# Re-ordering a hand-written five-engine schedule: loads, rotations and the last output unit of a fused attention and expert kernel

## The reference

```
h = layernorm(x)
q, k = rope(bf16(h @ Wq.T)), rope(bf16(h @ Wk.T))         # one head, width 128
o = sum over keys <= query of exp(q . k / sqrt(128))      # one number a row
a = relu(o @ fc1_w.T + fc1_b) @ fc2_w.T + fc2_b           # 1 -> 16 -> 128
x = x + layernorm(a)
h = layernorm(x)
y = relu(h @ W1[1] + b1[1]) @ W2[1] + b2[1]               # 128 -> 256 -> 128
x = x + layernorm(y)
```

## Time and profile before

| | us |
|---|---|
| median of 3 runs | 92.8 |
| lowest, highest | 92.72, 94.83 |
| the profiled execution | 92.89 |
| its span in the trace | 91.1 |

### The profile page before, as it was taken

How to read it: one execution, slowest core, us unless ns; L and a number is a source line. 1 busy time by engine, 2 the same in 40 slices (tenths; PEclk the granted TensorE clock), 3 DMA queues, 4 the chain that set the end, 5 groups by cost and what they waited for, 6 DMA issues and landing times.

```text
span 91.1 us, 1515 instructions
## 1 busy us (share of the span) xinstructions
PE 82.2 (90%) x439; PEld 49.2 (54%) x443; DVE 78.9 (87%) x210; ACT 67.7 (74%) x190; POOL 56.8 (62%) x79
## 2 busy tenths in 40 slices
...
GB/s 42 289 256 272 270 179 161 207 146 67 164 11 85 122 23 0 102 17 0 0 0 0 0 0 7 0 0 0 0 7 7 115 0 0 0 0 89 286 262 169
DMA packets 11852, 7.64 MB, mean 84 GB/s; under 512 B 819, under 2 KB 10948, under 8 KB 11844
## 3 DMA queue, kind: packets, MB, share of 16 engines
...
## 4 chain that ended last, share of the span: by engine, by line
PE 54%; ACT 23%; SPq 9%; DMA 5%; issue 2%; DVE 1%; POOL 1%; POOLq 1%; DVEq 0%
ACT psum L549 18%; PE psum L719 17%; PE psum L791 15%; PE psum L745 10%; DMA x_s<-x 5%; PE psum L711 5%; SPq L324 4%; PE psum L770 3%; SPq L304 2%; ACT fc L562 1%; PE psum L764 1%; ACT qk L501 1%; ACT h1T L518 1%; PE psum L749 1%; PE psum L781 1%
## 5 line engine op out<-in xcount | busy, mean ns | idle before, releaser
L485 POOL TENSOR_TENSOR rstd<-ve,half_neg 128x4 f32<-128x4 f32 (+1 forms) x36 | 35.7, 997 | 27.9 <-DVE ve L350 17.7
L549 ACT ACTIVATE psum<-psum 128x1024 f32<-128x1024 f32 (+7 forms) x48 | 36.5, 761 | 0.6 <-PE psum L749 0.2
L745 PE MATMUL psum<-qk_r 128*128 128x512 bf16 (+3 forms) x76 | 19.7, 346 | 1.8 <-ACT psum L549 1.3
L719 PE MATMUL psum<-cols_n,wqk 128*128 128x512 f32 (+1 forms) x36 | 16.9, 561 | 0.0
L719 PE MATMUL psum<-cols_n,w_c 128*128 128x512 f32 (+1 forms) x36 | 15.9, 551 | 0.0
L791 PE MATMUL psum<-w_c,hid 128*128 128x128 f32 x128 | 15.8, 276 | 0.0
L791 PEld LDWEIGHTS psum<-w_c,hid 128*128 128x128 f32 x128 | 15.3, 192 | 0.7 <-issue 0.3
L745 PEld LDWEIGHTS psum<-qk_r 128*128 128x128 bf16 x80 | 6.6, 97 | 12.9 <-ACT psum L549 6.3
L501 ACT ACTIVATE cols_n<-psum 128x512 f32<-128x512 f32 (+1 forms) x12 | 6.3, 528 | 8.2 <-PE psum L711 8.2
L711 PE MATMUL psum<-ident,rows_n 128*128 128x128 f32 x64 | 10.1, 276 | 0.9 <-DVE rows_n L344 0.9
L711 PEld LDWEIGHTS psum<-ident,rows_n 128*128 128x128 f32 x64 | 7.4, 141 | 5.9 <-issue 3.3
...
## 6 DMA issues: line engine op xcount, KB each, us to landing
x_s<-x SPq DMA_DIRECT2D x7, 256.0 KB, 4.3
qk_swap<-qk SPq DMA_DIRECT2D x14, 128.0 KB, 2.3
out<-x_s SPq DMA_DIRECT2D x7, 256.0 KB, 2.4
table<-tables SPq DMA_DIRECT2D x3, 256.0 KB, 3.8
x_s<-x SPq DMA_DIRECT2D x2, 128.0 KB, 3.2
w_f<-w SPq DMA_DIRECT2D x2, 128.0 KB, 3.7
table<-tables SPq DMA_DIRECT2D x2, 128.0 KB, 4.4
out<-x_s SPq DMA_DIRECT2D x2, 128.0 KB, 2.0
```

Source lines behind the costliest of these rows:

```text
L485: ready[k].done(eng.tensor_tensor(rstd[:, g, STAT_SLOT[k], t], ve[:, g, STAT_SLOT[k], t], half_neg[:, 0:tiles], ALU.pow), n)
L549: exps.done(eng.activation(area, area, ACT.Exp, scale=scale_qk, accum_out=sums[:, g, s, j:j + 1]), n, j, s)
L719: made[name].done(eng.matmul(bank_of(name, n)[:, 0:tiles * P], weight, cols_n[:, g, c], start=True, stop=True), n)
L745: mm = eng.matmul(psum[:, own[0] + i, 0:width], query, qk_r[:, g0 + c, 1, 0:width], start=True, stop=c < gb)
```

## The change

- Front unit 1 (second half of group 0) is no longer swapped by PE (`rot.1`) but by two transfers (`swap.1`). `rot.0` stays.
- A new list `OUTS` gives the units of the last stage (`y`, `bias`, `stat5`, `eps5`, `rstd5`, `ys`, `out`, `store`). It is BACKS, with unit 8 (two tiles) cut into units 8 and 9 of one tile. A `y` unit waits for the copies of the BACKS unit that holds its tile.
- `load_fc`, until now two issues on ACT's queue, goes to SP's queue, and the small loads take other places in it.
- STEPS is a new order for all engines, with other banks, and with some shared steps on other engines. `rot` apart, all arithmetic is the same.
- Branches for one tile to a bank are added to `net_pair`, `xs`/`ys` and `fc2`; no unit of the new STEPS gives a bank to one tile of several, so none of them runs.

```diff
+OUTS = [(0, 0, 4), (1, 0, 4), (4, 0, 4), (5, 0, 4), (2, 0, 4), (6, 0, 4), (3, 0, 4), (7, 0, 2), (7, 2, 1), (7, 3, 1)]
...
-load_x.0 blank.9#7 blank.1.128#7 load_x.3 repeat.0 load_x.4 mask.0 load_fc.0.A load_b1.0 load_wqk.0 stat1.0 load_x.1
-eps1.0.A rstd1.0 load_x.8 stat1.3 load_w2.0 norm1.0.D eps1.3.D load_x.6 stat1.4 tr1.0#0 rstd1.3 load_x.5 wqk.0#1
-eps1.4.D +tr1.0.A stat1.1 load_table.0 fc.0#2 rstd1.4 +wqk.0.A norm1.3.D load_b2.0 blank.1.128#7 q.0#1 eps1.1.D
-load_table.1 rstd1.1 tr1.3#0 norm1.4.D load_table.2 k.0#3 +tr1.3.A stat1.8 tr1.4#4 load_x.7 w2mean.0 stat1.6 q.3#0
-load_x.2 eps1.8.P +q.0.A stat1.5 +k.0.A eps1.6.P k.3#5 +tr1.4.A rstd1.6 cos.0.D w2.0 norm1.1.D rot.0#4 q.4#3 +k.3.D
-fcmean.0 norm1.6.P +q.3.A sin.0.D b2mean.0 tr1.1#1 swap.3 k.4#5 eps1.5.A rstd1.8 rope.0.D +q.4.A cos.3.D +tr1.1.A
-tr1.6#4 +k.4.A stat1.2 scores.0.1.0#1 norm1.8.P k.1#3 +tr1.6.A swap.4 scores.0.0.0#5 stat1.7 q.1#0 eps1.2.A +k.1.A
-q.6#4 rstd1.2 +fc.0 cos.4.D load_table.3 sin.3.D tr1.8#3 load_table.4 exp.0.1.0 k.6#6 rstd1.5 load_w1.0 rope.3.D
...
-stat5.1.D store.0 store.5 h1.7#2 store.3 eps5.1.D stat5.6.D rstd5.1 h0.7#3 store.4 +h1.7.D y.8#0 eps5.6.A +h0.7.D
-rstd5.6 out.1 y.7#3 stat5.8.A out.6 eps5.8.P store.1 stat5.7.A rstd5.8 eps5.7.D out.8 store.6 rstd5.7 store.8 out.7
-store.7
+load_x.0 blank.10#7 blank.1.384#7 load_x.3 repeat.0 load_x.6 mask.0 load_w2.0 load_wqk.0 stat1.0 load_x.4 eps1.0.A
+rstd1.0 stat1.3 load_x.8 load_x.5 eps1.3.D stat1.6 rstd1.3 load_fc.0 w2mean.0 norm1.0.D eps1.6.A wqk.0#0 norm1.3.D
+load_x.1 tr1.0#1 +wqk.0.A load_table.0 stat1.4 rstd1.6 blank.1.256#7 +tr1.0.A tr1.3#2 load_x.2 q.0#1 eps1.4.D stat1.8
++tr1.3.A rstd1.4 load_x.7 k.0#0 +q.0.A norm1.6.D blank.1.128#7 load_table.1 k.3#2 eps1.8.A w2.0 norm1.4.D load_b1.0
+q.3#1 load_table.4 +k.3.A rstd1.8 stat1.1 load_w1.0 stat1.5 eps1.1.A tr1.4#3 +q.3.A tr1.6#2 norm1.8.D +tr1.4.A swap.3
+fc.0#4 stat1.2 eps1.5.P +tr1.6.A rstd1.5 q.4#3 fcmean.0 load_b2.0 eps1.2.A cos.3.D +k.0.A tr1.8#2 load_table.2 cos.0.D
+k.4#0 +tr1.8.A stat1.7 norm1.5.P k.6#1 +q.4.D +k.4.A rstd1.1 sin.3.D +fc.0 swap.4 k.8#2 rstd1.2 rope.3.D rot.0#0
+b2mean.0 tr1.5#3 load_table.3 cos.4.D eps1.7.A b2.0 scores.2.3.0#4 +k.6.D norm1.2.P +tr1.5.A q.6#5 +k.8.A sin.0.D
+scores.2.0.0#1 norm1.1.P exp.2.3.0 scores.2.1.0#3 +q.6.D q.8#6 rstd1.7 exp.2.0.0 sin.4.D exp.2.1.0 swap.6 tr1.1#5
...
+eps3.0.D +trz.2.D rstd3.0 w1.0#1 cos.7.D exp.1.2.0 scores.5.2.0#67 +w1.0.D sin.7.P scores.4.3.1#2 x1.0 exp.5.2.0
...
+scores.4.2.1#2 eps3.7.D +trz.0.D scores.4.0.1#3 h0.3#4 rstd3.7 +hT.1 rope.7.P x1.7 scores.4.1.0#67 exp.4.0.1 exp.4.2.1
++h0.3.D fc2.1#15 exp.4.1.0 scores.5.0.0#23 stat3.1.D scores.5.1.1#4 h1.3#0 exp.5.1.1 eps3.1.D stat4.7 exp.5.0.0
+rstd3.1 sum.4.D scores.6.3.1#67 +h1.3.D h1.0#4 b2split.0 exp.6.3.1 x1.1 hT.4#0 scores.6.3.0#23 +hT.4 +h1.0.D
...
++h1.5.A eps5.3.P out.1 out.4.P trz.8#1 h0.6#3 +trz.8.A +h1.7.D +h0.7.D rstd5.3 y.5#1 store.4 +h0.6.A store.0 +h1.6.A
+out.2.P out.3 y.6#4 stat5.5.A store.2 store.3 store.1 eps5.5.A rstd5.5 h1.8#6 stat5.6.D h0.8#3 +h1.8.A out.5 y.7#2
+eps5.6.P +h0.8.A rstd5.6 y.8#3 store.5 stat5.7.D y.9#1 out.6 eps5.7.P stat5.8.A rstd5.7 stat5.9.A eps5.8.A eps5.9.A
+store.6 out.7 rstd5.8 rstd5.9 store.7 out.8 store.8 out.9 store.9
...
+OUT_STEPS = {"y", "bias", "stat5", "eps5", "rstd5", "ys", "out", "store"}
...
+        back_of = {(g, j): n for n, (g, j0, tiles) in enumerate(BACKS) for j in range(j0, j0 + tiles)}
...
-            g, j0, tiles = (FRONTS if name in FRONT_STEPS else BACKS)[n]
+            g, j0, tiles = (FRONTS if name in FRONT_STEPS else OUTS if name in OUT_STEPS else BACKS)[n]
...
-                    taken["h0"].wait(eng, n)
-                    taken["h1"].wait(eng, n)
+                    taken["h0"].wait(eng, back_of[g, j0])
+                    taken["h1"].wait(eng, back_of[g, j0])
```

More of the change, by code:

```diff
@@ L16 @@
 BLOCK = 32
-PAIR = 2 * BLOCK
 HIDDEN = 256
@@ L38 @@
 STEPS = """
[L39 to L73, removed]
@@ L74 @@
-+trz.8.A +h0.6.A rstd5.3 ys.4 h1.8#2 +h1.6.A h0.8#7 trz.7#0 out.0.P out.3 +h0.8.A y.6#6 +trz.7.A +h1.8.A out.4.P
-stat5.1.D store.0 store.5 h1.7#2 store.3 eps5.1.D stat5.6.D rstd5.1 h0.7#3 store.4 +h1.7.D y.8#0 eps5.6.A +h0.7.D
-rstd5.6 out.1 y.7#3 stat5.8.A out.6 eps5.8.P store.1 stat5.7.A rstd5.8 eps5.7.D out.8 store.6 rstd5.7 store.8 out.7
-store.7
+load_x.0 blank.10#7 blank.1.384#7 load_x.3 repeat.0 load_x.6 mask.0 load_w2.0 load_wqk.0 stat1.0 load_x.4 eps1.0.A
+rstd1.0 stat1.3 load_x.8 load_x.5 eps1.3.D stat1.6 rstd1.3 load_fc.0 w2mean.0 norm1.0.D eps1.6.A wqk.0#0 norm1.3.D
```

57 lines of the change are left out of this document (49 added, 8 removed).

## The result

The new kernel takes 95.5 us (median of four runs, 95.18 to 95.64), the old one 92.84. The ratio is 1.0268, 95% interval 1.0223 to 1.0314: 2.5 us slower, where I had forecast 0.8 faster.

What follows compares the result with a forecast made beforehand. Bound by the head, 22.5 us of ACT and DVE together, 47 us of PE and a tail: 92.89 - 0.6 (handover) + 0.2 (`rope.7`) - 0.3 (tail) = 92.2, rounded to 92.0 as median; range 90.3 to 94.4.

Steps and rivals of the forecast that it cites:

- the stretch bound by ACT and DVE: Before PE takes over near 39 us: gain at the handover 0.6 us, bounds -2.0 and +1.5.
- meetings: DVE products slowed beside POOL work on SBUF data, 0.82 us each; 0 to 3 more allowed, less than one taken.
- The slower rival: Six additional POOL rotation instructions hold up DVE products, 0.82 us each; four give 95.3; chance 0.15 including a late b2.
- The start of exp: Head: first exp at 17.3 against 16.88, ACT work 10.5 us against 9.2, waiting 0.8 to 0.9 us less.
- the lead of 0.8 us: ACT ahead in its sum through less waiting in the head; shows only as far as DVE leads too, 0.5 us.
- PE's stretch: From about 39 us on: PE full, same work, only waits can differ; 0.2 us taken, bounds 0 to 1.0.
- `rope.7`: Rotation step now on POOL, ready at 49.5 when PE wants scores at 49.7; cost 0.2 us, bounds 0 to 1.0.
- signs of being wrong: ACT waiting for b2, long DVE rotation rows, PE idle near 50, last matmuls beyond 86.5 or before 84.5.
- The tail: After the last matmul: nothing gained on engines, a smaller last transfer gives -0.3 us, bounds -0.6 to +0.3.

Runs made afterwards that it cites:

- old, norms in 4: Old kernel with each norm on POOL cut into one instruction per tile; ratio 1.0080 to the old kernel.
- old, more powers: Old kernel with an unread four-column power added behind each of the five norm1 steps on POOL; ratio 1.0132 to the old kernel.
- old, more products: Old kernel with an unread 128x512 product added behind each of the five norm1 steps on POOL; ratio 1.0423 to the old kernel.
- new, last unit whole: New kernel with the last output unit as one of two tiles again; 95.77 us, ratio 1.0242 to the old kernel.
- new, rotation on DVE: New kernel with cos.1, cos.5, sin.7 and rope.7 moved from POOL to DVE; 95.8 us, ratio 1.0227 to the old kernel.
- new, norms on DVE: New kernel with norm1.5, norm1.2, norm1.1 and norm4.2 moved from POOL to DVE; 95.14 us, ratio 1.0167 to the old kernel.
- new, norms in 4, `rot.1`: New kernel with POOL's norms cut by tile and unit 1 swapped by PE again, sin.1 moved ahead of +q.2; ratio 1.0113 to the old kernel.
- new, norms in 2: New kernel with each norm on POOL in two instructions of two tiles; ratio 1.0002 to the old kernel.
- new, norms in 4, old loads: New kernel with POOL's norms cut by tile and the first loads as in the old kernel; ratio 0.9994 to the old kernel.
- new, norms in 4, old loads, tail: New kernel with POOL's norms cut by tile, the old first loads, and eps5.8 ahead of stat5.9 on ACT; ratio 0.9989 to the old kernel.
- new, all wide steps cut: New kernel with POOL's norms cut by tile and its rotation steps in pieces of 256 columns; ratio 0.9988 to the old kernel.
- new, norms in 4: New kernel with each norm on POOL cut into one instruction per tile; ratio 0.9986 to the old kernel.

## Why the prediction was wrong

| kernel | holds, us | ratio |
|---|---|---|
| old | 0.8 | 1 |
| old, norms in 4 | 0.6 | 1.0080 |
| old, more powers | 1.2 | 1.0132 |
| old, more products | 5.4 | 1.0423 |
| new | 3.6 | 1.0268 |
| new, last unit whole | 3.4 | 1.0242 |
| new, rotation on DVE | 2.4 | 1.0227 |
| new, norms on DVE | 1.0 | 1.0167 |
| new, norms in 4, `rot.1` | 0.8 | 1.0113 |
| new, norms in 2 | 0.64 | 1.0002 |
| new, norms in 4, old loads | 0.5 | 0.9994 |
| new, norms in 4, old loads, tail | 0.5 | 0.9989 |
| new, all wide steps cut | 0.55 | 0.9988 |
| new, norms in 4 | 0.55 | 0.9986 |

Holds aren't all that sets the time: norms on DVE add 2.1 us of DVE work, rotation on DVE 2.2, and cuts and powers add POOL time.

**The step that failed** is in the stretch bound by ACT and DVE: "I allow 0 to 3 meetings more, and take less than one". There were four more, outside even my bounds: five holds against one, 2.8 us more. The mechanism was on the table, with the row of 1.24 us, with DVE at 15.26 of 15.40, and with the price of a meeting, 0.82 (the five measured 0.41 to 0.96, mean 0.71). The count was wrong. I set it by the old trace, where one product was long. But a count of meetings is a matter of what runs beside what, and the change set all of that anew. An old trace shows what a meeting costs and can't show how many a new order will have, so one meeting or two belonged into the middle of the sum, and more than three into its bounds.

**The slower rival** had the mechanism, the bound of DVE and nearly the time: "four meetings give 95.3", measured 95.5. It had the wrong holder, and the near hit of the time is in part luck. It counted the six additional rotation instructions of POOL; four of the five holds came from norms, of which POOL had eight, one fewer than before, but others and elsewhere. Moving the rotation steps back didn't help. And its 95.3 starts from 92.0, with gains that didn't come, and takes 0.82 for a meeting instead of 0.71; the two errors are opposite.

**The start of exp** was mis-sized too. I said 17.3; it is 18.90. No hold stands in it, as ACT works without a wait from 15.04 on:

```profile
14.18 0.60 ACT L505 ACTIVATE cols_n<-psum 128x512 f32<-128x512 f32 x1 [0.55 <-PE psum L716]
...
15.04 0.60 ACT L505 ACTIVATE qk<-psum 128x512 bf16<-128x512 f32 x1 [0.26 <-PE psum L724]
...
18.90 0.60 ACT L553 ACTIVATE psum<-psum 128x512 f32<-128x512 f32 x1
```

`+k.3` came at 10.36 instead of 9.5, and the waits after it were 0.8 us, not 0.2. The stretches tell what was wrong in the sum. Up to the first exp ACT was busy for 10.1 us in the old kernel (1.58 before 5.6 us, then 3.98 + 4.61) and for 12.3 in the new one (1.58, then 4.68 + 4.05, then 2.0 from 16.9 on): 2.1 us more, where I had summed 10.5 - 9.2 = 1.3. What wasn't ACT work was 6.7 us before and 6.6 after, where I had forecast 0.8 to 0.9 less. So the earlier loads of x gave nothing here, and the lead of 0.8 us that carried the forecast was never there. This fits with the new order without its holds being level with the old one (0.9986, whose interval leaves out my 92.0, a ratio of 0.991), but no run sets the head apart, so that part is argued and not shown. `b2mean`, which I had feared, waited for nothing. `sin.1`, which I had said to take alike from SBUF and PSUM, takes 0.42 us in the new kernel, where the old one took 0.68.

**PE's stretch.** From 63 us on it was full, as predicted, but the forecast rested on its being full from 39, and there it waited 1.1 us instead of 0.3, for an exp, for `x1` and for `hid`; the chain reached PE for good at 48.02 and not at 38.7. These waits are how DVE's lateness reaches the end. `rope.7` ended at 53.46 (POOL, 51.20 + 2.26), when PE was in `h1.3`; no wait. I had taken 0.2. Of my signs of being wrong, long rotation rows on DVE and a last matmul beyond 86.5 came true.

**The tail** came out within its bounds. New kernel:

```profile
88.83 0.66 PE L798 MATMUL psum<-w_c,hid 128*128 128x128 f32 x4
...
90.15 1.07 POOL L489 TENSOR_TENSOR rstd<-ve,half_neg 128x1 f32<-128x1 f32 x2 [0.24 <-ACT ve L602]
...
91.25 0.35 DVE L664 SCALAR_TENSOR_TENSOR x_s<-psum,rstd,x 128x128 f32<-128x128 f32 x1 [0.17 <-POOL rstd L489]
```

Last matmul 89.49, last `out` 91.60: 2.11 us, where I had 2.3, since a one-tile power takes 0.55 us, not 0.6, and begins earlier. From there to the end of the span 2.0, before 2.3. In all 4.1 against 4.6: -0.5, forecast -0.3.

**The sum as it came out:** four more holds 2.8 and the tail -0.5 make 2.3 us, against 2.5 between the two profiled executions (92.89 and 95.41). The sum takes each hold at its full length; 0.2 us stay open.

The Trainium skill (SBUF — State Buffer, "SBUF: two separate sides") gives the rule that I weighed and then priced too low: an exclusive lock between VectorE and GpSimd, for the whole instruction of whoever starts first. The runs agree with it in both directions for wide instructions, by the 5.4 us of holds with added products. They don't agree for every GpSimd instruction that reads SBUF: the power of a few columns, 1 us long, let a product run at 16.05, and not one of the 48 holds stands behind a power.
